# A fused eight-stage block: its first mixture of experts, dense over all experts, is done on rows sorted by expert

## The reference, cut to what matters

```python
x = x + L0_ffn(L0_cond(x, cond_8))      # x: 32 batches of 256 rows of 256 numbers, fp32
x = x + L1_ffn(L1_cond(x, cond_8))

def L0_ffn(x):                           # 32 x 256 = 8192 rows
    h = x + gqa(rmsnorm(x, attn_norm_w), wq, wk, wv, wo)     # causal, 16 heads, 4 key/value heads
    t = rmsnorm(h, ffn_norm_w)
    logits = t @ gate_w.T                # 8 experts
    w, sel = top_k(logits, 2); w = softmax(w)
    comb = sum(w[..., None] * one_hot(sel, 8), axis=1)
    out = 0
    for e in range(8):
        out = out + comb[:, e, None] * (t @ expert_w[e].T)   # 256 x 256 each
    return h + out
```

## Time and profile before

| | |
|---|---|
| median of three runs | 2656.84 us (2655.8 to 2663.13) |
| the profiled execution | 2656.05 us, of which the span from first to last instruction 2654.4 us |
| mean granted clock of TensorE | 0.959 of full speed |
| busy: PE / DVE / ACT / POOL | 2405.7 / 1529.6 / 1048.6 / 724.0 us |
| DMA | 222.11 MB, mean 84 GB/s |

### The profile page before, as it was taken

How to read it: one execution, slowest core, us unless ns; L and a number is a source line. 1 busy time by engine, 2 the same in 40 slices (tenths; PEclk the granted TensorE clock), 3 DMA queues, 4 the chain that set the end, 5 groups by cost and what they waited for, 6 DMA issues and landing times. The chain is left out here.

```text
span 2654.4 us, 50676 instructions
## 1 busy us (share of the span) xinstructions
PE 2405.7 (91%) x17352; PEld 1983.9 (75%) x17352; DVE 1529.6 (58%) x3200; ACT 1048.6 (40%) x2073; POOL 724.0 (27%) x782
## 2 busy tenths in 40 slices
PE   6999888999999996999999699999966999999997
PEld 6999755655556563788888499999965788888786
DVE  6887655655555564777777445555555434444442
ACT  6666544544455453111111133333323444444442
POOL 0000022222222221111111111222113555655654
PEclk9999999999999998999999799999987999999998
DMA  6666312111111111111111112222213434434533
GB/s 233 242 240 241 139 44 106 41 35 38 38 42 39 37 38 44 56 59 59 59 59 59 48 52 79 79 79 79 71 45 88 101 75 103 101 77 99 107 75 41
DMA packets 90255, 222.11 MB, mean 84 GB/s; under 512 B 13216, under 2 KB 32032, under 8 KB 83744
## 3 DMA queue, kind: packets, MB, share of 16 engines
q1 hardware_dynamic: 55328, 153.36, 17.0%
q0 software_dynamic: 34816, 67.13, 11.2%
HBM read 161.20 MB, written 58.72 MB: 83 GB/s over the span
## 5 line engine op out<-in xcount | busy, mean ns | idle before, releaser
L708 DVE TENSOR_REDUCE neg_max<-ring 128x2 f32<-128x512 f32 (+1 forms) x384 | 241.2, 684 | 76.4 <-PE ring L825 76.4
L1947 POOL DMA_INDIRECT out<-eo,row_put x128 | 202.0, 1578 | 242.9 <-ACT eo L2010 213.7
L612 POOL TENSOR_SCALAR_AFFINE_SELECT weights_diag<-weights_diag 128x512 f32<-128x512 f32 x256 | 154.0, 637 | 370.0 <-ACT weights_diag L649 370.0
L1203 DVE SCALAR_TENSOR_TENSOR acc<-expert_ps,comb,acc 128x256 f32<-128x256 f32 x512 | 209.5, 477 | 37.5 <-PE expert_ps L60 36.8
L58 PE MATMUL expert_ps<-we_lo,n_hi 128*128 128x512 f32 x512 | 211.1, 412 | 0.1
L60 PE MATMUL expert_ps<-we_hi,n_hi 128*128 128x512 f32 x512 | 202.5, 396 | 0.0
L59 PE MATMUL expert_ps<-we_hi,n_lo 128*128 128x512 f32 x512 | 202.4, 395 | 0.0
L2085 DVE TENSOR_TENSOR ex_hid<-ex_up_ps,gelu 128x512 f32<-128x512 f32 x128 | 87.0, 690 | 186.6 <-ACT gelu L1994 186.6
L1936 POOL DMA_INDIRECT toks<-hs,row_get x128 | 157.1, 1227 | 74.3 <-issue 38.4
L649 ACT ACTIVATE weights_diag<-ring 128x512 f32<-128x512 f32 x256 | 132.7, 602 | 92.3 <-PE ring L841 92.3
L1994 ACT ACTIVATE gelu<-ex_gate_ps 128x512 f32<-128x512 f32 x128 | 76.3, 596 | 201.3 <-PE ex_up_ps L60 201.3
(11 more groups left out here) (272 smaller groups left out, 7500.2 us busy)
## 6 DMA issues: line engine op xcount, KB each, us to landing
ug_raw<-in_w_ug SPq DMA_DIRECT2D x32, 1028.0 KB, 5.0
dn_raw<-in_w_dn SPq DMA_DIRECT2D x32, 640.0 KB, 6.0
expert_gu<-in_expert_gu SPq DMA_DIRECT2D x16, 1024.0 KB, 4.9
x_raw<-in_x_t SPq DMA_DIRECT2D x32, 256.0 KB, 5.0
c<-c_sb POOLq DMA_DIRECT2D x32, 256.0 KB, 5.1
c0n<-c SPq DMA_DIRECT2D x32, 256.0 KB, 2.7
c0r<-c SPq DMA_DIRECT2D x32, 256.0 KB, 2.7
expert_d<-in_expert_d SPq DMA_DIRECT2D x16, 512.0 KB, 6.0
```

The lines of the kernel that those rows point to most:

```text
L612: nc.gpsimd.affine_select(part, part, [[0, G], [1, P]], ALU.is_ge, 0.0, base=0, channel_multiplier=-1).then_inc(kept_done, 1)
L708: nc.vector.tensor_reduce(out, src, AX_X, ALU.max, negate=True).then_inc(max_done, 1)
L1203: nc.vector.scalar_tensor_tensor(out=acc[par][:, t, :], in0=expert_ps[(TT * m + t) % EBANKS][:, c, :], scalar=comb[par][:, t, 2 * m + c:2 ...
L1947: nc.gpsimd.indirect_dma_start(out=out_rows, out_offset=bass.IndirectOffsetOnAxis(ap=at, axis=0), in_=eo[c][:, n, :], in_offset=None, comp ...
```

## The change

`moe_phase` is gone. Its routing moves into the attention stage, and each row is computed with its two chosen experts alone.

- Attention: the output projection moves from step i-1 on `piece_b` to step i-2 on `piece_a`; at i-2 the second norm follows (squares and scaling on ACT, root on POOL, now one root for both norms), at i-3 its transposes and the gate, at i-4 and i-5 the top-two choice, a count of earlier rows of the same expert (products with a triangular matrix and with ones, `prefix`), and the row number in the region of each chosen expert. POOL writes the rows into these regions with four indirect transfers a batch (`scatter`) and adds x to h (`add_x`). The unrolled steps are now -3 to 7 and 28 to 36, the loop is 8 to 27.
- At its end DVE works out which expert each of 136 tiles of 128 rows belongs to (`list_tiles`, 15 instructions in a chain), and SP clears what the last tile of each expert reads beyond its rows (`clear_ends`). The high and low parts of the expert weights are made in the last four steps.
- New stage `sorted_tiles_phase`: 68 steps of two tiles. SP loads two tiles from rows whose numbers it reads from SBUF, PE turns them, ACT and DVE make high and low parts, PE multiplies each with the weights whose column it reads from SBUF (2 x 2 x 3 = 12 products of 256 columns), ACT empties them, POOL stores them.
- `lora_shared_phase`: POOL gathers the two result rows of every row (four indirect transfers a batch), DVE adds them, weighted, to the sum (`combine`, four instructions) and computes `weff_low`, which POOL did. SP stores x1 and loads it again.
- The first stage loads seven more small constants.

In the diff the new functions stand in the order SP, POOL (attention), SP, PE (new stage), POOL, DVE (linear layer).

```diff
-STEADY = (4, 28)
+STEADY = (8, 28)
...
-        A_ORDER = (("values_q1", -1), ("heads_q0", -1), ("heads_q1", -1), ("q_a", 2), ("q_b", 2), ("values_q0", 0))
-        B_ORDER = (("shift_q0", 0), ("norm_t", 2), ("kv", 2), ("out_t", -1), ("shift_q1", 1), ("out_proj", -1))
+        A_ORDER = (("values_q1", -1), ("heads_q0", -1), ("heads_q1", -1), ("out_proj", -2), ("q_a", 2), ("q_b", 2), ("values_q0", 0))
+        B_ORDER = (("shift_q0", 0), ("norm_t", 2), ("kv", 2), ("norm2_t", -3), ("shift_q1", 1), ("out_t", -1), ("prefix", -4), ("gate", -3))
...
+            def clear_ends():
+                sp.wait_ge(list_step, 15)
+                for e in range(EM):
+                    at_ = sp.value_load(free_row[0:1, e:e + 1], min_val=0, max_val=EM * REGION - P)
+                    sp.dma_start(sorted_rows[bass.ds(at_, P), :], zeros[:]).then_inc(zeros_out, 16)
+                sp.wait_ge(zeros_out, 16 * 2 * EM)
...
+            def scatter(b):
+                pool.wait_ge(row_step, times(ROWS, b, 3))
+                alone(pool)
+                for t in range(TT):
+                    for n in range(2):
+                        to = bass.IndirectOffsetOnAxis(ap=row_now[b[1] % 2][:, t, n:n + 1], axis=0)
+                        nc.gpsimd.indirect_dma_start(out=sorted_rows, out_offset=to, in_=n2[b[1] % 4][:, t, :], in_offset=None).then_inc(scattered[b[1] % 2], 16)
+
+            def add_x(b):
+                pool.wait_ge(a_free, per_a("out_proj", later(b, 2)) + 1)
+                pool.wait_ge(x_in[b[1] % 4], 16 * turn4(b) + 16)
+                nc.gpsimd.tensor_tensor(x_sb[b[1] % 4][:], x_sb[b[1] % 4][:], h_sb[b[1] % 2][:], ALU.add).then_inc(sum_done, 1)
...
+def sorted_tiles_phase(nc, sem, sorted_rows, results, routes, ident):
+    STEPS = TILES0 // 2
...
+            def body(s):
+                n = s[1] % 4
+                for c in range(2):
+                    at_ = sp.value_load(routes.tile_row[0:1, bass.ds(2 * number(s, 0) + c, 1)], min_val=0, max_val=SORTED - P)
+                    if c == 0:
+                        until(sp, turned_done, number(s, -3))
+                        alone(sp)
+                    sp.dma_start(rows_sb[n][:, c, :], sorted_rows[bass.ds(at_, P), :]).then_inc(rows_in[n], 16)
...
+            def products(s):
+                p = s[1] % 2
+                columns = [pe.value_load(routes.tile_column[0:1, bass.ds(2 * number(s, 0) + c, 1)], min_val=0, max_val=(EM - 1) * D) for c in range(2)]
+                pe.wait_ge(lo_done, number(s, 1))
+                until(pe, kept_done, number(s, -1))
+                for c, column in enumerate(columns):
+                    own = bass.ds(column, D)
+                    for k in range(KT):
+                        last = exact_product(nc, product[p][:, c, :], (t_hi[p][:, c, k, :], t_lo[p][:, c, k, :]),
+                                             (routes.we_hi[:, k, own], routes.we_lo[:, k, own]), k == 0, k == KT - 1)
+                last.then_inc(product_done, 1)
+
+            def body(s):
+                if not is_last(s):
+                    turn(ahead(s, 1))
+                products(s)
...
             def body(j, par, has_prev, has_next):
+                if not (isinstance(j, int) and j == PAIRS - 1):
+                    gather(j + 1, par)
                 if has_next:
-                    weff_low(*after(j, par))
                     store_hs(*after(j, par))
...
+            def combine(j, par):
...
+                for n in range(2):
+                    for t in range(TT):
+                        if n:
+                            dve.wait_ge(x1_step, 4 * i + t + 1)
+                        alone(dve)
+                        nc.vector.scalar_tensor_tensor(out=x1_sb[par][:, t, :], in0=picked[par][:, 2 * t + n, :],
+                                                       scalar=routes.share[:, bass.ds(2 * TT * i + 2 * t + n, 1)],
+                                                       in1=(x1_sb if n else sum_sb)[par][:, t, :], op0=ALU.mult, op1=ALU.add).then_inc(x1_step, 1)
```

More of the change, by code:

```diff
@@ L1229, in _ @@
+            over_steps(dve, close_rows, low)
         @block.tensor
         def _(pe):
[L1231 to L1239 removed]
```

1013 lines of the change are left out of this document (625 added, 388 removed).

## The result

The changed kernel takes 2876.8 us (median of four runs, 2870.8 to 2879.4) against 2656.3 for the kernel before: 1.0821 times as long (95% interval 1.0796 to 1.0846). The prediction was 2608, with a range that ended at 2705. It was wrong in size and in sign.

What follows compares the result with a forecast made beforehand. PE was taken to bound experts, attention and linear layer. From 2656.05 us: -424 + 200 + 106 - 7 + 3.3 + 3 + 20 + 47 + 4 = -47.7, giving 2608 us; range of 8 in 10 from 2515 to 2705.

Steps and rivals of the forecast that it cites:

- POOL is not late: Attention: POOL's scatters, earlier work and addition of x sum to 14.3 us a step, under the step's 23.4.
- the port's rule: Attention: DVE instructions with two SBUF inputs exclude GpSimd's SBUF reads; each could wait for a select, step some 0.5 us longer.
- if POOL's scatters hold anything up: Closing sign: the prediction is wrong if POOL's scatters delay anything, or tile steps lie outside 2.3 to 3.7 us.
- The step's own terms: Attention: 1.7 us of added PE work and 1.6 of waits take a step from 20.06 to 23.4 us, +106 in all.
- (b): Attention: the queries now wait for DVE's residual, 3.7 us against PE's 3.1 of work between; wait 0.6 a step.
- (a): Attention: four or five added DVE instructions push the norm's remainder; PE's keys and values wait 0.4 us a step.
- (d): Attention: the prefix products wait for the remainder of the turned heads, 0.3 us a step.
- rival B: Sorted tiles: PE's clock stays at 1.2 GHz, a step takes 4.9 us, +136, total 2744 us; chance 0.10.
- The +47: Linear layer: DVE's `combine` and `weff_lo` add 1.5 us a batch through later `b_lo` and `weff_lo`, times 31.
- The term for `weff_lo`: Linear layer: computed on DVE after its own remainder, `weff_lo` ends about 0.9 us later relative to `weff`.
- the prediction's side sentence: Tiles: with the skill's 600 ns a read, a step would be 1.9 us on SP and 3.3 in series on PE.
- Rival C: Attention and linear layer: DVE becomes the bound, 173 and 84 us instead of 106 and 47, total 2712; chance 0.10.

Runs made afterwards that it cites:

- gather_ahead: weff_first with POOL's gathers in the linear layer started one batch further ahead, behind DVE's `weff`: 2672.6 us.
- scatter_last: Changed kernel with POOL's four scatters of an attention step issued at the end of its body instead of the head: 2691.8 us.
- scatter_middle: Changed kernel with POOL's four scatters in attention behind the eight selects and ahead of the addition of x: 2700.5 us.
- filler_products: Changed kernel with 16 useless PE products a batch in the linear layer, where PE waits for x1: 2835.8 us.
- combine_early: Changed kernel with DVE's four `combine` instructions ahead of `add_bias` instead of at the body's end: 2809.6 us.
- weff_first: combine_early with DVE's `weff_lo` ahead of the hidden rows' remainder instead of behind it: 2780.7 us.
- orders_again: Changed kernel with scatters last, `combine` before `add_bias`, `weff_lo` before the hidden rows' remainder, PE's reads before the transposes; repeated in another comparison: 2592.4 us, first 2549.2.
- rows_by_sp: Changed kernel with POOL's scatters in attention replaced by plain SP transfers of as much data to fixed places: 2696.0 us.

## Why the prediction was wrong

**Attention: the sentence on POOL failed, as a price.** "POOL is not late: [...] under 23.4 and in an order that ends before its result is needed" is true of POOL's results: PE waited for a select once. But, the port's rule aside (below), it is all that the prediction asked of POOL, and the sum took nothing for it. It left out that POOL's queue decides beside which of DVE's instructions its work falls. The scatter at the head waits for row numbers that DVE makes in the middle of the step; behind it the selects come as one block, beside the cast and the maxima for which PE waits. The prediction's own last sign, "if POOL's scatters hold anything up", came true. Moving the scatter alone took a step from 28.4 to 23.0 us, and 177 of the 254 up to the last residual. The split of these 5.4 us a step is less sure. Gather_ahead has the scatters at the head and not the wait before `k_t`, and takes 26.4: that gives 2.0 to the wait and 3.4 to DVE held beside the selects, with the clock in both. There DVE's `gap` is held and PE waits for the residual in its place:

```profile
PE piece_a L58 <- DVE h_sb L932: 43.1, 14, 4.3
```

**The step's own terms** were somewhat too high. A step with the order mended is 2.0 us above before (23.0 against 21.0) where 3.3 were predicted. From 600 to 900 us PE is busy for 276.2 us in scatter_last and for 284.5 before, which over 13.0 and 14.3 steps is 1.3 us more a step (an estimate, since some records are missing; 1.7 predicted), and idle for 0.7 more (1.6 predicted). Its waits in scatter_last are 0.3 for the values, 0.2 for the residual, 0.3 for the maxima (0.2 before, too) and 0.2 for the mask a step: under half of what (b) gave the queries, and nothing for (a) and (d). The whole of attention then is 77 us longer than before, against +105.

**A term was missing:** the output projection moved from one body after its scores to two (`("out_proj", -1)` to `-2`). The last residual is 69.6 us behind the last copy of the queries, before 49.0. That drain of a step, 12 us in scatter_last and 21 here, is paid once. That the moved projection makes it is read from the order; no run moved it back.

**The port.** The prediction weighed the exclusion of DVE and GpSimd (the Trainium skill, "SBUF — State Buffer", section "Who interferes with whom") at 0.5 us a step, for instructions with two SBUF inputs. The same section of the Trainium skill says that copies, casts and `tensor_scalar` can contend too, and the trace agrees: the cast of `picked` takes 1.85 us (median of 21 steps, up to 2.55) beside the selects, and `odds` 0.88 beside POOL's addition of 1.28, 0.89 in scatter_last; in scatter_middle, where it does not meet the addition, it takes 0.16. And where in gather_ahead a two-input instruction, `gap`, met the selects, it stood until near their end (DVE, then POOL):

```profile
745.02 3.62 DVE L951 TENSOR_TENSOR gap<-top 128x2 f32<-128x2 f32 x1
748.56 0.68 DVE L872 TENSOR_REDUCE neg_max<-ring 128x2 f32<-128x512 f32 x1
```

```profile
744.47 4.74 POOL L721 TENSOR_SCALAR_AFFINE_SELECT weights_diag<-weights_diag 128x512 f32<-128x512 f32 x8
```

"Held up to a select" was too little: the subtraction got through only when seven of the eight selects had passed. That section of the Trainium skill speaks of a lock for one instruction; what the row shows is longer, and the row decides.

**The clock.** No term was kept for it outside rival B, which put it in the tiles, where it stood at 0.99. It fell in the two stages where it had been 0.96 and 0.99, and new pauses of 2.2 us had appeared in both. For the linear layer filler_products shows that the pause is the cause, and prices it at about 1.4 us a batch, 45 us. In attention the row at 0.57 gives about 2.7 us a step by the estimate above; there the pause was not filled by itself, so the cause is argued from the linear layer.

**The linear layer: a reader was missed.** The +47 counted what `combine` delays behind it (`b_lo`, `weff_lo`) and not who needs its result: PE's transposes of x1 come right behind the routing products. Its 2.17 us wait, and the clock, are combine_early's 62 us of stage. The term for `weff_lo`, 0.9 a batch, was of about the right size (weff_first: 36 us over 31.6 batches, 1.1, across two comparisons). With both orders mended and without the waits that have no releaser the stage is 432.7 us, as before the change (433.3): the gathers and DVE's four instructions are then free, and the lower bound of 19 was still too high.

**The tiles.** 3.26 us a step against 2.9, inside 2.3 to 3.7. The mis-sized thing is what hides PE's reads: nothing does, 0.6 us each. By the floor of about 600 ns that the Trainium skill gives for a `tensor_load` ("DMA: Bandwidth & Descriptors", section "Latency and other measured facts") the prediction's side sentence had 3.3 a step in series on PE, which is what came; the sum's 0.82 a read, from SP's issues, was too high and its hiding too hopeful, and the two errors in part cancelled.

**The handover** was 49.7 us against 42.5; 45.7 in scatter_last. It was not taken apart. Nor were the 7 us behind the linear layer.

**The waits without releaser** were foreseen by nothing. From gather_ahead those before `k_t` are worth 2.0 us a step here, 62 us in attention. What they are is open. In the changed kernel and in orders_again they end about 1 us behind POOL's last indirect transfer of a group. But rows_by_sp, where POOL issues none in attention, doesn't single these out: scatter_last has no such wait beside its scatters either (both have 2.7 us in three waits, all before 400 us). In the changed kernel's step PE's own products, too, stood 0.22 and 0.44 us at 730.2 and 730.9 with nothing waited for. What holds the instructions back, and why not in one comparison, no run here can say.

**The chances.** Rival C had the right sign and its two stages, by another mechanism (DVE's length), and ended 165 us short, so its sign was luck. The range failed because each upper bound priced instructions end to end, and none priced a queue or a clock.

## To carry to other kernels

When an instruction that waits is added to an engine's queue, list what stands behind it, who needs that, and beside which instructions of other engines it will now run, before adding up busy times; and for each result that an added instruction makes, find its first reader. Give every new pause of PE of about 2 us the price of the slow products behind it as well. Changing only the order of four calls turned a kernel 8% slower than before into one 2.4 to 4.0% faster.

## What the runs showed of the hardware

- In attention PE's pause of 2.2 us was followed by 7.5 us at a granted clock of 0.57. In the linear layer a pause of 2.2 us a batch stood beside a clock of 0.88; filled with useless products it left the clock at 1.00 and the batch 1.4 us shorter.
- DVE's cast of 128x4 numbers took 0.16 us alone and 1.8 to 2.5 beside POOL's selects; a subtraction of 128x2, 0.15 alone, took 3.60 (median of 23) beside them.
- PE reads a register from SBUF in about 0.6 us (two reads, 1.2 us), and behind twelve queued products the two cost as much (3.22 us a step against 3.26).
- The same program took 2549.2 us on one chip and 2592.4 on another, while the kernel before took 2656.3 and 2653.0 there. The stage of the linear layer accounts for 38 of the 43 us, with waits of about 3 us before `sh_hid` that end some 1 us behind POOL's indirect transfers, for PE's work that is recorded as ended.
